# Linear attention and routed experts: the first LayerNorm's statistics move from VectorE to ScalarE

## The chip, the cores and the metric

The kernel runs on one core of a Trainium2 chip (trn2). The metric is device time in microseconds (us); the time before is the median of three runs. PE is TensorE, DVE is VectorE, ACT is ScalarE, POOL is GpSimd and SP is SyncE, whose queue issues most transfers.

## What is computed

The input x has 8 sequences of 512 tokens and 256 features. In short:

```
def _layernorm(x, axis=-1, eps=1e-05):
    m = jnp.mean(x, axis=axis, keepdims=True)
    v = jnp.var(x, axis=axis, keepdims=True)
    return (x - m) / jnp.sqrt(v + eps)
...
    x = L0_attn_x
    x = x + _L0_attn_ref(_layernorm(x, axis=-1), ...)
    x = x + _L0_ffn_ref(_layernorm(x, axis=-1), ...)
    return x
```

The attention is a causal linear one: q, k and v are projected, phi(z) = elu(z) + 1 is taken of q and k, running sums of k*v and of k decay with a constant for each head, and q times the first is divided by the sum over the head of q times the second; then comes the output projection. The second part routes each token to 4 of 32 small gated experts and adds one shared expert. The change concerns the LayerNorm ahead of the attention only.

## The kernel before

The kernel has two phases. The first is a software pipeline of nine steps, b = 0 to 8, written out by hand (`steps(step)` on each engine). In step b the engines do, for one sequence each: the attention of sequence b (`st.now`), the output projection, second LayerNorm and router of sequence b-1 (`st.before`), the placing of the rows of sequence b-2 in lists for the experts (`st.past`), and the first LayerNorm of sequence b+1 (`st.after`, steps 0 to 6). Before step 0 the first LayerNorm of sequence 0 is done alone. Beside it three experts' weights are turned in each step: PE transposes them into three PSUM banks in turn, ACT copies the high half out, DVE the low half (`prep_in`, `prep_out`; L720 and L875). The second phase runs tiles of 128 rows through the experts (32 of the shared expert and 159 of routed ones), and a last part adds three partial sums and stores the output. The change touches nothing behind the first phase.

Every engine works through its own list in order; semaphores tie the lists together. A sequence is held as 128 partitions x 4 tiles (TS = 4) x 256 features.

The first LayerNorm of sequence b+1 before the change: at the top of its step DVE runs `bn_stats` on four tiles (L798) and `bn_aggr` four times (L801), with two small writes between that carry waits (L315), and writes the variance plus epsilon (`vare`, L805) and minus the mean (`less`, L807). POOL raises the variance to the power -0.5 (L573) and multiplies by `less` (`shift`, L577); that is `root(0, b+1)`. ACT then writes the normalised rows `xn` in four instructions (L706, `norm_in`), PE transposes them (L1129, `xn_in`) and ACT copies the result out as `xnT` (L711, `xn_out`). The next step's projections (L1261) start from it.

What stands around it in the order of the lists, for a step b with all parts:

- ACT: exp and relu of k, feature half 0 (L726, L727); the spread of the inverted denominators (L743); the same two of q (L733, L734); `share_out` (L698); `norm_in(b+1)` (L706); the issue of the load of x for sequence b+2 (L756); k and q, half 1, and the copies of the turned weights.
- DVE: statistics of b+1; `choose` (L965, L967); the attention output (L890); `count_rows` (L973 to L979); phi of half 0 (L851, L853), the scan (L859) and k*v (L865); the residual sum (L903, once for each half of the rows); the second LayerNorm's statistics (L798 again); `rank_picks` (L989 on), weights (L875), the second LayerNorm itself (L823), the split of its rows (L845), and the second half of the attention with its scans (L870) and the inversion (L835, L837); router selection (L947, L950).
- PE: denominators (L1361), q projection, transposes of the spread denominators (L1285), v projection, output projection (L1296, 16 matmuls, which wait for L890), then K, Q and V of half 1 with weight transposes between (L1139 to L1144), `xn_in`, more weights, the next K, and the router's transposes and matmuls (L1330, L1348).
- POOL: in steps 3 to 8 it issues the indirect transfers that put rows in the experts' lists (L586), in fixed numbers between its other work: 3, then `root(0, b+1)`, 3, then q*ksum (L562), 2, then `root(1, b-1)` for the second LayerNorm (L573 again), and more around the two products q*kvsum (L566).
- SP: the store of the residual rows, which the second LayerNorm waits for, and the loads of the next experts' weights (L366 to L370), for which the first weight transpose of a step waits.

Of the kernel before, what the change touches and what calls it, by code (L numbers as in the profile page):

```python
# [5 lines left out]
def moe_block(nc, x, w_qkv, w_out, decay_param, router_w, router_b, gate_w, up_w, down_w,  # L6
              shared_gate_w, shared_up_w, shared_down_w, w_late, out):
    f32, f16, i32, u32 = mybir.dt.float32, mybir.dt.float16, mybir.dt.int32, mybir.dt.uint32
    ALU = mybir.AluOpType
# [3 lines left out]
    P = 128  # L13
# [3 lines left out]
    TS = S // P  # L17
# [31 lines left out]
    with ctx:  # L49
        def sb(name, shape, dt):  # L50
            return ctx.enter_context(nc.sbuf_tensor(name, shape, dt))
# [4 lines left out]
        def sem(name):  # L56
            return ctx.enter_context(nc.semaphore(name))
# [98 lines left out]
        idx8 = sb("idx8", [P, TS, 8], u32)  # L156
        carrier = sb("carrier", [P, 1], f32)
        iota_i = top8[:, :, :].rearrange("p j k -> p (j k)").bitcast(i32)
        iota_e = sb("iota_e", [P, E], f32)
# [21 lines left out]
        row_experts = payload[:, :, EXP_AT // 2 - H:EXP_AT // 2 - H + K]  # L181
        share_sum = sb("share_sum", [P, TS], f32)
        mhalf = sb("mhalf", [P, TS], f32)
        stats = [sb(f"stats{n}", [P, TS, 6], f32) for n in range(2)]
        mv = [sb(f"mv{n}", [P, TS, 2], f32) for n in range(2)]
        vare = [sb(f"vare{n}", [P, TS], f32) for n in range(2)]
# [32 lines left out]
        setup_dve = sem("setup_dve")  # L219
        ln_stats = [sem(f"ln_stats{n}") for n in range(2)]  # L220
        ln_aggr = [sem(f"ln_aggr{n}") for n in range(2)]
        ln_vare = [sem(f"ln_vare{n}") for n in range(2)]
# [89 lines left out]
        def wait_apart(eng, semaphore, value):  # L312

            eng.wait_ge(semaphore, value)
            nc.vector.memset(carrier[:, :], 0.0)  # L315
# [329 lines left out]
        def _(act):  # L645
# [49 lines left out]
            def share_out(b):  # L695

                act.wait_ge(share_shifted, b + 1)
                nc.scalar.activation(shares, shares, ACT.Exp).then_inc(share_exp, 1)  # L698

            def norm_in(b):  # L700

                act.wait_ge(ln_shift, b + 1)
                if b >= 1:
                    act.wait_ge(xn_transposed, HC * b)
                for j in range(TS):
                    nc.scalar.activation(xn[:, j], x_sb[b % 2][:, j], ACT.Identity, bias=shift[:, j:j + 1], scale=rstd[0][:, j:j + 1]).then_inc(xn_ready, 1)  # L706
# [29 lines left out]
            def step(st):  # L736
                b = st.b
                if st.now:
                    k_parts(b, 0)
                if st.before:  # L740

                    act.wait_ge(den_inverted, b)
                    nc.scalar.activation(attn_words.rearrange("p (n d) -> p n d", d=D), rden[:, :].unsqueeze(2).to_broadcast([P, TS * HEADS, D]), ACT.Copy).then_inc(rden_spread, 1)  # L743
                if st.now:
                    q_parts(b, 0)
                if st.past:
                    share_out(b - 2)
# [35 lines left out]
                if st.now:  # L783
                    for n in range(6, 9):
                        prep_out(b, n)

            norm_in(0)
            xn_out(0)
# [6 lines left out]
        def _(dve):  # L795
            def norm_stats(n, src, b):
                for j in range(TS):
                    nc.vector.bn_stats(stats[n][:, j], src[:, j]).then_inc(ln_stats[n], 1)  # L798
                wait_apart(dve, ln_stats[n], TS * b + TS)
                for j in range(TS):  # L800
                    nc.vector.bn_aggr(mv[n][:, j], stats[n][:, j]).then_inc(ln_aggr[n], 1)  # L801
                if n == 0 and b >= 1:
                    dve.wait_ge(ln_shift, b)
                wait_apart(dve, ln_aggr[n], TS * b + TS)
                nc.vector.tensor_scalar(vare[n][:, :], mv[n][:, :, 1], LN_EPS, None, ALU.add).then_inc(ln_vare[n], 1)  # L805
                if n == 0:
                    nc.vector.tensor_scalar(less, mv[0][:, :, 0], -1.0, None, ALU.mult).then_inc(ln_less, 1)  # L807

            dve.wait_ge(x_loaded[0], 16)
            norm_stats(0, x_sb[0], 0)  # L810
            dve.wait_ge(setup_act, 4)
# [7 lines left out]

            def norm(n, dst, src, b, done):  # L820
                dve.wait_ge(ln_rstd[n], b + 1)
                for j in range(TS):
                    nc.vector.tensor_scalar(dst[:, j], src[:, j], mv[n][:, j, 0:1], rstd[n][:, j:j + 1],  # L823
                                            ALU.subtract, ALU.mult).then_inc(done, 1)
# [52 lines left out]
            def step(st):  # L877
                b = st.b
                if st.after:
                    dve.wait_ge(x_loaded[(b + 1) % 2], 16 * ((b + 1) // 2 + 1))  # L880
                    norm_stats(0, x_sb[(b + 1) % 2], b + 1)
                if st.past:
# [8 lines left out]
                if st.past:  # L891
                    count_rows(b - 2)
                if st.now:
                    phi(b, 0)
                    k_sum(b, 0)
                    k_times_v(b, 0)
                if st.before:
# [7 lines left out]
                    dve.wait_ge(x1_done, 2 * b)  # L905
                    norm_stats(1, x1_sb, b - 1)
                if st.past:
# [8 lines left out]
                if st.before:  # L916
                    dve.wait_ge(x1_stored, 16 * b)
                    norm(1, xn2, x1_sb, b - 1, xn2_ready)
                if st.now:
# [489 lines left out]
```

## Time and profile before

| | |
|---|---|
| median of 3 runs | 755.38 us (753.37 to 756.12) |
| span of the profiled execution, first to last instruction | 707.9 us |
| what the median has around that span | 47.5 us |
| PE busy | 603.2 us (85%) |
| DVE busy | 512.6 us (72%) |
| ACT busy | 434.9 us (61%) |
| POOL busy | 440.3 us (62%) |

The spans come from one execution that the hardware profiler recorded; no separate device time of that execution is given, so its span stands beside the median. Busy shares are averages over both phases. In the first phase, up to about 280 us, the engines take turns in waiting for each other, and what one of them saves counts only where the chain of waits goes through it.

### The profile page before, as it was taken

The numbers are of one execution on the slowest core, as the hardware profiler recorded it, in microseconds if no ns is written. First come the engines' busy times: TensorE is split into PE (matmuls) and PEld (weight loads), VectorE is DVE, ScalarE is ACT, GpSimd is POOL, SyncE is SP. The second block draws the span as 40 slices with busy tenths as digits, with TensorE's granted clock in tenths as the row PEclk, the third lists the DMA queues.
The fourth block names the chain that finished last, engine by engine and source line by source line (L and its number), as shares of the span: only waits on it lengthen the run. The fifth ranks groups of instructions, "written<-read, shape, count | busy, mean of one in ns | idle before, by whom it ended". The sixth has DMA issues, their size and how long they took to land.

```text
span 707.9 us, 15496 instructions
## 1 busy us (share of the span) xinstructions
PE 603.2 (85%) x4725; PEld 417.4 (59%) x4725; DVE 512.6 (72%) x1966; ACT 434.9 (61%) x1045; POOL 440.3 (62%) x367
## 2 busy tenths in 40 slices
PE   3898877897888899899999999999999999999000
PEld 2565544565555565677777777776777777776000
DVE  2588898989889968877766666666666666666164
ACT  2646445463636433688878878787788878788000
POOL 3031148658585776777078778887888888888300
PEclk9989999899999969999999999999999999999555
DMA  9664585959667676999589889888988888886799
GB/s 275 265 182 120 160 240 176 301 194 271 197 203 226 202 229 205 302 335 336 164 148 144 139 140 143 140 141 140 143 140 149 140 140 142 141 145 91 189 412 385
DMA packets 121460, 140.41 MB, mean 198 GB/s; under 512 B 22626, under 2 KB 110210, under 8 KB 120834
## 3 DMA queue, kind: packets, MB, share of 16 engines
q1 hardware_dynamic: 88816, 97.29, 44.4%
q0 software_dynamic: 29040, 38.68, 33.1%
q10 hardware_dynamic: 3522, 3.44, 1.5%
q8 instruction: 40, 0.66, 0.4%
q14 instruction: 42, 0.34, 0.2%
HBM read 79.19 MB, written 64.89 MB: 204 GB/s over the span
## 4 chain that ended last, share of the span: by engine, by line
PE 60%; DVE 19%; issue 6%; DMA 6%; POOL 4%; SPq 3%; ACT 2%; POOLq 0%; ACTq 0%; DVEq 0%
PE psD L1245 13%; PE psQ L1212 11%; PE psK L1212 11%; PE psT L1183 6%; PE psD L1296 4%; DMA acc_scratch<-arena 3%; DVE W L875 2%; DVE W L870 2%; SPq L514 2%; PE psK L1261 2%; PE psQ L1261 2%; DMA W<-acc_scratch 2%; PE psT L1232 2%; PE psV L1261 2%; PE psV L1232 2%
## 5 line engine op out<-in xcount | busy, mean ns | idle before, releaser
L640 POOL DMA_INDIRECT acc_scratch<-arena x159 | 251.3, 1581 | 73.2 <-issue 34.7
L586 POOL DMA_INDIRECT xlist_scratch<-list_row,dest x128 | 133.7, 1045 | 35.6 <-issue 34.1
L1245 PE MATMUL psD<-W,arena 128*128 (+1 forms) x955 | 135.5, 273 | 1.0 <-DVE arena L1044 0.9
L1048 DVE COPY arena<-psT 128x512 f16<-128x512 f16 x191 | 81.0, 424 | 69.2 <-PE psT L1183 68.6
L1212 PE MATMUL psK<-W,arena 128*128 (+1 forms) x576 | 109.3, 326 | 0.5 <-DVE arena L1048 0.5
L1212 PE MATMUL psQ<-W,arena 128*128 (+1 forms) x570 | 108.2, 326 | 0.1
L1245 PEld LDWEIGHTS psD<-W,arena 128*128 128x128 f16 x955 | 85.2, 98 | 8.0 <-DVE arena L1044 1.1
L671 ACT ACTIVATE arena<-arena 128x192 f16<-128x192 f32 x191 | 69.2, 362 | 13.9 <-DVE arena L1072 2.2
L680 ACT ACTIVATE arena<-psD,arena 128x256 f32<-128x256 f32 x159 | 72.8, 458 | 3.4 <-DMA acc_scratch<-arena 3.1
L1183 PE MATMUL psT<-ident,arena 128*128 128x128 f16 x764 | 74.0, 220 | 0.4 <-issue 0.4
L1183 PEld LDWEIGHTS psT<-ident,arena 128*128 128x128 f16 x764 | 57.0, 98 | 29.3 <-issue 7.2
L1091 DVE TENSOR_TENSOR arena<-arena 128x64 f16<-128x64 f32 x191 | 43.0, 225 | 40.4 <-ACT arena L671 40.4
L1212 PEld LDWEIGHTS psK<-W,arena 128*128 128x128 f16 x576 | 50.6, 97 | 33.7 <-DVE arena L1048 1.1
L1212 PEld LDWEIGHTS psQ<-W,arena 128*128 128x128 f16 x570 | 50.1, 97 | 32.4 <-DVE arena L1048 0.2
L566 POOL TENSOR_TENSOR W<-W 128x512 f32<-128x512 f32 x16 | 20.3, 1270 | 71.4 <-DVE W L870 71.3
L1092 DVE TENSOR_TENSOR arena<-arena 128x128 f16<-128x128 f32 x191 | 54.4, 285 | 0.0
L668 ACT ACTIVATE arena<-psT 128x384 f16<-128x384 f16 x95 | 46.6, 490 | 10.0 <-PE psT L1232 5.6
L668 ACT ACTIVATE arena<-psV 128x384 f16<-128x384 f16 x96 | 47.0, 490 | 7.4 <-PE psV L1232 2.1
L875 DVE SCALAR_TENSOR_TENSOR W<-psT,W 128x384 f16<-128x384 f32 (+1 forms) x72 | 40.0, 588 | 13.6 <-ACT W L720 13.6
L1296 PE MATMUL psD<-W 128*128 128x256 f32 x128 | 36.3, 447 | 11.6 <-DVE W L890 11.5
L720 ACT ACTIVATE W<-psT 128x384 f16<-128x384 f32 (+1 forms) x72 | 35.6, 528 | 16.5 <-PE psT L1139 8.5
L664 ACT ACTIVATE arena<-psK 128x192 f32<-128x192 f32 x96 | 31.7, 330 | 20.4 <-PE psK L1212 20.0
(164 smaller groups left out, 1084.8 us busy)
## 6 DMA issues: line engine op xcount, KB each, us to landing
arena<-xlist_scratch SPq DMA_DIRECT2D x159, 136.0 KB
W<-acc_scratch SPq DMA_DIRECT2D x24, 512.0 KB, 12.7
acc_scratch<-arena SPq DMA_DIRECT2D x16, 512.0 KB, 5.9
arena<-in_L_attn_x_dram SPq DMA_DIRECT2D x10, 512.0 KB, 5.1
arena<-in_L_ffn_down_w_dram SPq DMA_DIRECT2D x23, 192.0 KB, 4.9
xlist_scratch<-pad_scratch SPq DMA_DIRECT2D x32, 136.0 KB, 3.6
list_row<-xrow_scratch SPq DMA_DIRECT2D x32, 136.0 KB
acc_scratch<-arena SPq DMA_DIRECT2D x33, 128.0 KB, 12.4
```

Source lines behind the costliest of these rows:

```text
L586: nc.gpsimd.indirect_dma_start(xlist[:, :], bass.IndirectOffsetOnAxis(ap=dest[:, n:n + 1], axis=0), list_row[j % LISTS][:, :], None).then_ ...
L640: nc.gpsimd.indirect_dma_start(acc[t % ACCS][:, :], bass.IndirectOffsetOnAxis(ap=token[:, (t - NT) % DEEP:(t - NT) % DEEP + 1], axis=0), y ...
L668: nc.scalar.activation(aT[u].rearrange("p n t -> p (n t)"), psA[u], ACT.Copy).then_inc(aT_done, 1)
L671: nc.scalar.activation(halves[t % 2][:, 0:I], act32[t % 2], ACT.Copy).then_inc(a_hi_done, 1)
L680: nc.scalar.activation(y_sb[(t - 2) % ROUND], psY[t % 2], ACT.Copy, scale=share[:, (t - 2 - NT) % DEEP:(t - 2 - NT) % DEEP + 1]).then_inc( ...
L875: nc.vector.scalar_tensor_tensor(dst, bank_of("prep", n)[:, 0:width], WS, hi, ALU.mult, ALU.subtract).then_inc(prep_lo, 1)
L1048: nc.vector.tensor_copy(xT[t % 2].rearrange("p s c t -> p (s c t)"), psX[t % 2]).then_inc(xT_done, 1)
L1092: nc.vector.tensor_tensor(both[:, 2 * P:3 * P], act32[t % 2][:, 0:P], both[:, 0:P], ALU.subtract).then_inc(a_split, 1)
L1183: last = nc.tensor.transpose(psX[t % 2][:, n * P:(n + 1) * P], xg[t % XG][:, n * P:(n + 1) * P], ident16[:, :])
L1212: last = nc.tensor.matmul(psG[t % 2][:, 0:GU], xT[t % 2][:, sx, h], weights(t, (2 * h + sw) * GU, GU), start=(n == 0), stop=(n == 3 * HC - 1))
L1245: last = nc.tensor.matmul(psY[u], aT[u][0:height, part], weights(t - 2, GUW + q * H, H, height), start=(n == 0), stop=(n == len(parts) - 1))
L1296: last = nc.tensor.matmul(psD[:, j // 2, (j % 2) * H:(j % 2 + 1) * H], attnT[:, c, j * P:(j + 1) * P], wout_sb[:, c, :], start=(c == 0), s ...
```

## The change

ACT now makes the statistics of the first LayerNorm. `sum_in` copies each tile of x into `xn`, used as scratch, and lets ACT's accumulator add it up (four instructions); DVE turns the sums into minus the mean (`mean_in`, one operation on 128 x 4). `square_in` squares x minus the mean with the accumulator on (four instructions); DVE turns these into variance plus epsilon (`variance_in`, one operation). POOL's two operations and ACT's `norm_in` stay. The second LayerNorm keeps `bn_stats` on DVE.

In the lists, ACT gets `sum_in(b+1)` between L727 and L743 and `square_in(b+1)` between L734 and L698; DVE has `mean_in(b+1)` at the top of the step, where the statistics stood, and `variance_in(b+1)` behind `count_rows`, ahead of phi. For sequence 0 all four parts stand in front of everything else of the pipeline, on ACT behind the four set-up operations L652 to L655.

```
+            def sum_in(b):
+                act.wait_ge(x_loaded[b % 2], 16 * (b // 2 + 1))
+                if b >= 1:
+                    act.wait_ge(xn_transposed, HC * b)
+                    act.wait_ge(ln_less, b)
+                for j in range(TS):
+                    nc.scalar.activation(xn[:, j], x_sb[b % 2][:, j], ACT.Copy, accum_out=x_sum[:, j:j + 1]).then_inc(x_summed, 1)
+
+            def square_in(b):
+                act.wait_ge(ln_less, b + 1)
+                if b >= 1:
+                    act.wait_ge(ln_vare[0], b)
+                for j in range(TS):
+                    nc.scalar.activation(xn[:, j], x_sb[b % 2][:, j], ACT.Square, bias=less[:, j:j + 1],
+                                         accum_out=x_square[:, j:j + 1]).then_inc(x_squared, 1)
...
                 if st.now:
                     k_parts(b, 0)
+                if st.after:
+                    sum_in(b + 1)
                 if st.before:
...
                 if st.now:
                     q_parts(b, 0)
+                if st.after:
+                    square_in(b + 1)
...
+            sum_in(0)
+            square_in(0)
             norm_in(0)
...
+            def mean_in(b):
+                if b >= 1:
+                    dve.wait_ge(ln_shift, b)
+                    dve.wait_ge(xn_ready, TS * b)
+                dve.wait_ge(x_summed, TS * b + TS)
+                nc.vector.tensor_scalar(less, x_sum, -1.0 / H, None, ALU.mult).then_inc(ln_less, 1)
+
+            def variance_in(b):
+                dve.wait_ge(x_squared, TS * b + TS)
+                if b >= 1:
+                    dve.wait_ge(ln_rstd[0], b)
+                nc.vector.tensor_scalar(vare[0][:, :], x_square, 1.0 / H, LN_EPS, ALU.mult, ALU.add).then_inc(ln_vare[0], 1)
...
-            dve.wait_ge(x_loaded[0], 16)
-            norm_stats(0, x_sb[0], 0)
+            mean_in(0)
+            variance_in(0)
...
                 if st.after:
-                    dve.wait_ge(x_loaded[(b + 1) % 2], 16 * ((b + 1) // 2 + 1))
-                    norm_stats(0, x_sb[(b + 1) % 2], b + 1)
+                    mean_in(b + 1)
...
                 if st.past:
                     count_rows(b - 2)
+                if st.after:
+                    variance_in(b + 1)
                 if st.now:
                     phi(b, 0)
```

## Rows read from the trace of the kernel before

**Rows 1.** The chain that ended last, step 4: start, us, what.

```profile
134.38 1.30 DVE stats L798 x4
136.64 1.20 DVE W L890 x2
151.24 0.79 DVE arena L823 x3
```

**Rows 2.** PE's timeline, steps 2, 3, 4: start, us, engine, line, shape, [idle before <-releaser].

```profile
73.96 5.34 PE L1296 MATMUL psD<-W 128*128 128x256 f32 x16 [2.19 <-DVE W L890]
81.28 0.49 PE L1139 MATMUL psT<-ident,arena 128*128 128x128 f32 x3
...
105.03 3.72 PE L1296 MATMUL psD<-W 128*128 128x256 f32 x16 [2.20 <-DVE W L890]
...
133.81 1.88 PE L1261 MATMUL psV<-W 128*128 128x512 f32 x4
137.88 5.41 PE L1296 MATMUL psD<-W 128*128 128x256 f32 x16 [2.19 <-DVE W L890]
```

**Rows 3.** Stretches: us, PE, PEld, DVE, ACT, POOL busy, PEclk, DMA share, GB/s.

```profile
140.00:141.00 1.00, 1.00 (x4) 0.81 (x3) 1.00 (x2) 1.00 (x3) 0.78 (x1) 0.50 0.68 252
252.00:256.00 4.00, 4.00 (x17) 3.19 (x16) 0.62 (x1) 0.00 (x0) 3.79 (x4) 0.50 0.12 37
```

**Rows 4.** ACT's timeline, steps 2 and 4.

```profile
67.84 1.06 ACT L743 ACTIVATE W<-W 128x1024 f32<-128x1024 f32 x1 [1.99 <-DVE W L837]
...
131.76 1.06 ACT L743 ACTIVATE W<-W 128x1024 f32<-128x1024 f32 x1 [1.53 <-DVE W L837]
139.98 0.60 ACT L706 ACTIVATE W<-arena,W,rstd 128x256 f32<-128x256 f32 x1 [3.17 <-POOL W L577]
```

**Rows 5.** POOL's timeline, step 4, and DVE's in step 3.

```profile
138.22 1.12 POOL L573 TENSOR_TENSOR rstd<-vare,mhalf 128x4 f32<-128x4 f32 x1
147.69 1.04 POOL L573 TENSOR_TENSOR rstd<-vare,mhalf 128x4 f32<-128x4 f32 x1
...
119.93 1.54 DVE L823 TENSOR_SCALAR arena<-arena,mv,rstd 128x256 f32<-128x256 f32 x4 [2.04 <-POOL rstd L573]
```

**Rows 6.** Groups by line and shape: x count, busy us, mean ns, idle before.

```profile
L680 ACT ACTIVATE arena<-psD,arena 128x256 f32<-128x256 f32 x159 | 72.8, 458 | 3.4 <-DMA acc_scratch<-arena 3.1
L706 ACT ACTIVATE W<-arena,W,rstd 128x256 f32<-128x256 f32 x32 | 16.6, 592 | 19.2 <-POOL W L577 19.2
L1057 DVE DVE_READ_ACCUMULATOR arena<-arena 128x1 f32 x159 | 13.2, 83 | 0.0
L682 ACT ACTIVATE arena<-psD 128x256 f32<-128x256 f32 x32 | 11.8, 369 | 2.3 <-DMA acc_scratch<-arena 2.3
L698 ACT ACTIVATE payload<-payload 128x16 f32<-128x16 f32 x8 | 1.7, 216 | 18.4 <-DVE payload L965 18.4
```

**Rows 7.** Timeline of the start, before step 0.

```profile
6.89 0.17 DVE L805 TENSOR_SCALAR vare<-mv 128x4 f32<-128x4 f32 x1
8.33 0.20 POOL L577 TENSOR_TENSOR W<-W,rstd 128x4 f32<-128x4 f32 x1
9.96 0.24 ACT L655 ACTIVATE rwT<-psD 128x64 f16<-128x64 f32 x1
10.07 2.08 ACT L706 ACTIVATE W<-arena,W,rstd 128x256 f32<-128x256 f32 x4
```

**Rows 8.** Timeline of step 0.

```profile
19.23 0.59 ACT L727 ACTIVATE W<-psK 128x512 f32<-128x512 f32 x1
21.76 2.06 ACT L706 ACTIVATE W<-arena,W,rstd 128x256 f32<-128x256 f32 x4
```

**Rows 9.** DVE's timeline in step 1.

```profile
43.52 1.29 DVE L890 TENSOR_TENSOR W<-W,psD 128x512 f32<-128x512 f32 x2 [0.24 <-PE psD L1285]
```

**Rows 10.** SP's queue in step 2, and transfers of 62 to 82 us.

```profile
73.41 0.47 SPq L370 DMA_DIRECT2D arena<-in_L_ffn_down_w_dram  x1
...
arena<-in_L_ffn_down_w_dram SPq DMA_DIRECT2D x3, 64.0 KB, 4.7
```

More of the change, by code:

```diff
@@ L157, in moe_block @@
         carrier = sb("carrier", [P, 1], f32)
+        stats_words = sb("stats_words", [P, 2 * TS], f32)
         iota_i = top8[:, :, :].rearrange("p j k -> p (j k)").bitcast(i32)
@@ L182, in moe_block @@
         share_sum = sb("share_sum", [P, TS], f32)
+        x_sum, x_square = stats_words[:, 0:TS], stats_words[:, TS:2 * TS]
         mhalf = sb("mhalf", [P, TS], f32)
-        stats = [sb(f"stats{n}", [P, TS, 6], f32) for n in range(2)]
-        mv = [sb(f"mv{n}", [P, TS, 2], f32) for n in range(2)]
+        stats = sb("stats", [P, TS, 6], f32)
+        mv = sb("mv", [P, TS, 2], f32)
         vare = [sb(f"vare{n}", [P, TS], f32) for n in range(2)]
@@ L219, in moe_block @@
         setup_dve = sem("setup_dve")
-        ln_stats = [sem(f"ln_stats{n}") for n in range(2)]
-        ln_aggr = [sem(f"ln_aggr{n}") for n in range(2)]
+        ln_stats, ln_aggr = sem("ln_stats"), sem("ln_aggr")
+        x_summed, x_squared = sem("x_summed"), sem("x_squared")
         ln_vare = [sem(f"ln_vare{n}") for n in range(2)]
@@ L795, in _, with norm_stats @@
         def _(dve):
-            def norm_stats(n, src, b):
+            def mean_in(b):
[9 more added lines that the diff above has]
+                nc.vector.tensor_scalar(vare[0][:, :], x_square, 1.0 / H, LN_EPS, ALU.mult, ALU.add).then_inc(ln_vare[0], 1)
+            def norm_stats(src, b):
                 for j in range(TS):
-                    nc.vector.bn_stats(stats[n][:, j], src[:, j]).then_inc(ln_stats[n], 1)
-                wait_apart(dve, ln_stats[n], TS * b + TS)
+                    nc.vector.bn_stats(stats[:, j], src[:, j]).then_inc(ln_stats, 1)
+                wait_apart(dve, ln_stats, TS * b + TS)
                 for j in range(TS):
[L801 to L807, printed above, removed]
-            dve.wait_ge(x_loaded[0], 16)
-            norm_stats(0, x_sb[0], 0)
+                    nc.vector.bn_aggr(mv[:, j], stats[:, j]).then_inc(ln_aggr, 1)
+                wait_apart(dve, ln_aggr, TS * b + TS)
+                nc.vector.tensor_scalar(vare[1][:, :], mv[:, :, 1], LN_EPS, None, ALU.add).then_inc(ln_vare[1], 1)
+            mean_in(0)
+            variance_in(0)
             dve.wait_ge(setup_act, 4)
@@ L818, in _, with norm @@
             dve.wait_ge(setup_dve, 3)
-            def norm(n, dst, src, b, done):
-                dve.wait_ge(ln_rstd[n], b + 1)
+            def norm(dst, src, b, done):
+                dve.wait_ge(ln_rstd[1], b + 1)
                 for j in range(TS):
-                    nc.vector.tensor_scalar(dst[:, j], src[:, j], mv[n][:, j, 0:1], rstd[n][:, j:j + 1],
+                    nc.vector.tensor_scalar(dst[:, j], src[:, j], mv[:, j, 0:1], rstd[1][:, j:j + 1],
                                             ALU.subtract, ALU.mult).then_inc(done, 1)
@@ L905, in step @@
                     dve.wait_ge(x1_done, 2 * b)
-                    norm_stats(1, x1_sb, b - 1)
+                    norm_stats(x1_sb, b - 1)
                 if st.past:
@@ L917, in step @@
                     dve.wait_ge(x1_stored, 16 * b)
-                    norm(1, xn2, x1_sb, b - 1, xn2_ready)
+                    norm(xn2, x1_sb, b - 1, xn2_ready)
                 if st.now:
```

## The prediction

> **What bounds the kernel now.** I read the page first: PE is busy most and DVE next, but both are averages over two phases, and the change lies in the first. So I followed the chain of waits through that phase, then laid the timelines of PE, ACT, DVE and POOL of one step beside each other, and last asked for short stretches to see PE's granted clock.
>
> In step 4 the chain goes through the four `bn_stats` at the top of DVE's step, from 134.38, and reaches the attention output L890 at 136.64 [rows 1]. PE waits 2.19 us for it in front of the output projection, though its v projection (four matmuls of 0.43, so 1.72 of path) had begun at 133.81 and is over near 135.6 [rows 2]. From L1296 on PE is busy without a gap until the weights' transposes, and then the chain is DVE's again from the second LayerNorm L823 at 151.24 [rows 1] to the next step's statistics. So the statistics lie on the path, at 134.38 to 136.4. Steps 2, 5 and 6 read the same. Three steps differ. In step 1 DVE waits for PE before L890 [rows 9], so the statistics before it cost nothing. In step 3 POOL is last: L823 waits 2.04 us for POOL's root [rows 5]. Steps 7 and 8 have no first LayerNorm.
>
> A second effect lies on the same place. L1296 takes 5.34 and 5.41 us in steps 2 and 4 but 3.72 in step 3 [rows 2], and the clock granted at 140 to 141 is 0.50 [rows 3]: the 1.2 GHz level, granted for 3.4 us after PE had stood idle. The wait for DVE thus costs about 1.8 us more in steps 2, 4, 5 and 6.
>
> **The price of the new ACT operations.** No ACT instruction of the trace uses the accumulator. A tile of 128x256 costs 369 ns without a pointer operand, 458 with one (its scale), 592 with two [rows 6]. Four L706 in a row take 2.08 us [rows 7], or 0.50 each, so neighbours overlap by 0.1. A copy is then 0.28 and a square with its bias pointer 0.36, if reading the accumulator is hidden: the lower ends. If the read is an instruction of its own, the nearest rows are DVE's read, 83 ns, and a tiny ACT operation, 216 ns [rows 6]; with 216 and no overlap the copy is 0.59 and the square 0.67: the upper ends. I take a little above the middle, 0.45 and 0.54: a read without much to do, partly overlapped. Four and four make 1.8 and 2.2 us (1.1 to 2.4, and 1.4 to 2.7).
>
> The Trainium skill, ScalarE: Activation LUTs, section What ACT_TABLE_LOAD costs, gives 186 ns plus 0.833 per element, 93 more for a pointer operand, and an overlap of 93. By it a copy is 0.31 and a square 0.40, an estimate without the accumulator's read; the eight would be 2.8 us instead of my 4.0. The rows at 369 and 458 are near it (399 and 493), and it has no price for the read.
>
> **The start: +6.0 us.** Now DVE and POOL finish the statistics of sequence 0 at 8.53 under ACT's idle wait, and ACT goes from its set-up operation at 9.96 straight to L706 at 10.07 [rows 7]. With the change ACT can begin to sum only at 10.07, as its queue is in order. Then come 1.8 for the sums, 0.3 for `mean_in` with the hand-over both ways (an operation on 128x4 is 0.17), 2.2 for the squares, 0.25 for `variance_in`, and POOL's pair, 1.47 from L805's end to L577's end [rows 7]: 6.0 us until L706 can start. The cover that hid this work is gone, and PE has nothing else to do. Ends: 4.5 and 7.1.
>
> **Step 0: +2.5 us.** In it ACT goes from L727 at 19.23 over q to L706 at 21.76, without a wait for POOL [rows 8]. Now the sums run from 19.7 to 21.5, q to 22.5, squares to 24.7, DVE's variance to 25.0, POOL to 26.5, and `norm_in` starts 4.7 late. Queued behind it on ACT are k and q of half 1 and the weights' copies; queued behind `variance_in` on DVE is phi of half 0, so V of half 1 on PE waits too. PE's transposes of xn come about 1.9 late, ACT's copies of them and the next K 2.5 late; idle time of PE absorbs the rest. Ends: 1.1 and 3.6, as the eight prices change.
>
> **Step 1: 0.** It is PE-bound [rows 9]. The sums fit between L727 and L743, as PE and DVE are slower here. The squares end about 0.8 behind L890 and hold phi back by that; DVE waits for PE in L903 anyway.
>
> **Step 2: -2.8 us.** DVE loses 1.97 of statistics and gets `mean_in` for 0.1. PE's end is limited by the spread L743: ACT idles 1.99 in front of it, where step 4 has 1.53 [rows 4], and with the overlap of 0.1 the 1.8 of sums fit in. L1296 starts 1.9 earlier, with 0.3 of idle time before it. Then the 1.2 GHz stretch should not come, which gives 1.8 more. But then a transfer is in the way: the last weights are issued at 73.41 plus 0.47 and take 4.7 to land [rows 10], so 78.6, while the first weight transpose, L1139 at 81.28 now [rows 2], would come 3.7 earlier, at 77.6. It waits 1.0. So 1.9 + 1.8 - 1.0, near 2.8. Without the clock it is 1.9.
>
> **Step 3: 0.** POOL is last, and its list of work is the same; `variance_in` at about 104.5 is there before POOL asks for it.
>
> **Steps 4, 5, 6: -2.4 us each.** The sums push L743 back by 1.8 - 1.63 = 0.2 in step 4; PE still starts L1296 about 1.9 earlier. With the clock 3.7 would be free, but POOL is next: its second L573 ends at 147.69 + 1.04 = 148.73 [rows 5], and its chain of work up to there has no gap since DVE's scan at the end of the step before. L823 can go from 151.24 [rows 1] to 148.83, which is 2.4. Without the clock 1.9 counts in full. The squares run 134.6 to 136.8, DVE asks for them at 137.3, POOL for the variance at 138.22 [rows 5], and L706 stays near 139.98 [rows 4], ahead of the k it stands before. Ends of the price: at 0.67 a square the last is there at 137.3, still in time; at 0.59 a sum L743 is 0.7 late, and L1296 gains 1.5 before the clock.
>
> **Sum.** 6.0 + 2.5 - 2.8 - 7.2 = -1.5 us against the profiled span of 707.9, so 706.4. The median of the runs, 755.38, has 47.5 around that span, which the change doesn't touch: 753.9 us. With the low prices it is -1.5 - 1.5 - 1.4 = -4.4 (751.0), with the high ones -1.5 + 1.1 + 1.1 + 1.2 = +1.9 (757.3).
>
> **Rivals.**
> - *The clock stays low in the steps.* 6.0 + 2.5 - 4 x 1.9 = +0.9: 756.3. For it: the idle wait for L743 stays. Against: the low stretch came right behind the 2.19 of idle time, and that is what goes.
> - *The clock at the phase's end.* At 252 to 256 the granted clock is 0.50 while PE is wholly busy [rows 3]. PE fills and computes the last denominators there on the path, some 13 us of such work before the last residual sum; I estimate 5 of them to be the clock's, as L1296 loses 1.7 of 5.4 to it [rows 2] and this stretch is three times as long. Whether a drop falls there seems to hang on where the timeline lies. Shifted, it may not come: 753.9 - 5 = 749.
> - *The accumulator is dear (the other side).* If every accumulated instruction drains ACT, at 0.8 for a sum and 0.9 for a square, the start is 3.2 + 3.6 + 2.1 = 8.9, step 0 is 2.5 + 2.8 = 5.3, and L743 is pushed 1.1 late in steps 2, 5 and 6 and 1.6 in step 4, so that L1296 gains 1.1, 1.1, 1.1 and 0.6. Sum +10.3: 765.7. It turns the sign from a mean price of 0.59 on and shows as slower by over 0.5% from about 0.70. Against it: a tiny ACT operation is only 216 ns.
> - *The accumulator is free:* 751.0, above.
> - *Tables.* Square could need another activation table than Exp. The trace has one load of 1.3 us at the start and one in the second phase, so exp, relu and copies share one now. Two loads of 1.3 in each of eight LayerNorms, half of them hidden, would be +10: 764. The Trainium skill, ScalarE: Activation LUTs, section Table sets: the hidden batching unit, says that cheap functions are in every set and that a switch is about 2.7 us; by it sixteen switches would be 43 us of ACT, an estimate, if Square were no such function. No row here has a Square.
>
> **How the numbers follow.** Forecast 0.50; clock stays low in the steps 0.10; clock at the end comes back 0.15; accumulator free 0.10; accumulator dear 0.12; tables 0.03. A change within 0.5%, or 3.8 us, is about what a measurement here can't tell from none: 751.6 to 759.2. Faster: 0.15, and 0.06 of the free accumulator, and 0.04 of the forecast, make 0.25. Slower: 0.12 + 0.03 + 0.02 = 0.17. The rest, 0.58, is no change. The range runs from 747, below the end-clock case, to 760, above the high prices with the low clock; it leaves out the dear accumulator and the tables, 0.15.
>
> **What would show it.** Right: `norm_in(0)` starting at 16 instead of 10.07; step 0 some 2.5 longer; PE idle before L1296 near 0.3 in steps 2, 4, 5, 6 and its 16 matmuls near 3.6; L823 of steps 4 to 6 waiting for POOL's L573; four sums in 1.8 and four squares in 2.2. Wrong: L1285 waiting longer for L743 than its 0.75 to 1.5 of now; DVE waiting at `variance_in` in steps 2 to 6; table loads between the steps; another clock pattern in step 1 or 8, which alone can move the time by 3 to 5 us.

## The result, and the profile after

The changed kernel takes 757.39 us (20 runs, 751.26 to 761.04), the kernel before 750.38 (20 runs beside them, 744.66 to 756.12): a ratio of 1.0087, 95% interval 1.0061 to 1.0113, so it is slower by 6.5 us. The forecast was 753.9 and most likely no change; the range of 747 to 760 holds the time, the sign does not fit. That the range holds it is luck: the forecast started from 755.38, the median of three runs, where 20 runs give 750.38, and put the change at -1.5, where it is +6.5. Two errors of 5 and 8 us went against each other.

Two things about the comparison first. The profiled execution of after spans 759.2 us and its own time was 761.04, so only 1.8 us lie around a span (1.7 to 1.9 in every later run). The 707.9 of before was thus an execution near 710, and the 47.5 us that the forecast added were no constant. Chips differ: on some the kernel before takes 703 to 706 us, on others 750 to 752, nearly all of it in the first tiles of the second phase (last section). Ratios below are always against the kernel before on the same chip, and steps are compared in the first phase only, where the profiles of both kinds of chip show the same step lengths.

Each step is timed at the start of the second LayerNorm's normalisation (L823 before, L860 after), which stands in the last part of a step. The table has these starts in us, from the timelines of two executions of each kernel; the rows "later than before" are what the change had cost up to there:

```
step                     1       2       3       4       5       6       7       8
before, first         56.18   87.25  119.93  151.24  182.39  213.51  241.53  272.64
after, first          63.00   91.83  124.07  155.43  186.14  216.86  246.85  277.21
later than before      6.8     4.6     4.1     4.2     3.8     3.4     5.3     4.6
before, second        56.59   87.73  120.40  150.74  180.31  211.55  239.55  267.50
after, second         63.15   90.89  123.09  153.42  183.29  213.98  243.97  272.05
later than before      6.6     3.2     2.7     2.7     3.0     2.4     4.4     4.6
```

Both pairs tell one story: 6.7 lost until step 1, 2.2 and 3.4 won back in step 2, 1.2 and 0.7 in all of steps 3 to 6, and 2 lost again in step 7. The forecast ran +8.5 up to step 1, then -2.8, 0, three times -2.4, 0.

The start, after (timeline; the rows that answer to [rows 7] and [rows 8]):

```profile
9.92 0.44 ACT L709 ACTIVATE W<-arena 128x256 f32<-128x256 f32 x1
...
11.87 0.51 ACT L717 ACTIVATE W<-arena,W 128x256 f32<-128x256 f32 x1 [0.24 <-DVE W L828]
...
14.23 1.04 POOL L575 TENSOR_TENSOR rstd<-vare,mhalf 128x4 f32<-128x4 f32 x1 [9.10 <-DVE vare L835]
...
15.66 2.07 ACT L726 ACTIVATE W<-arena,W,rstd 128x256 f32<-128x256 f32 x4 [1.72 <-POOL W L579]
...
32.48 0.60 ACT L726 ACTIVATE W<-arena,W,rstd 128x256 f32<-128x256 f32 x1 [2.56 <-POOL W L579]
```

ACT starts to sum when it started to normalise before, and normalises 5.6 later, at 15.66. In step 0 the second row of L726 stands at 32.48; it was 21.76, so 10.7 later, 5.1 of it new.

The new operations, after: ACT's timeline at the start of step 5, and the groups (line, shape, count, busy, mean ns):

```profile
165.31 0.43 ACT L709 ACTIVATE W<-arena 128x256 f32<-128x256 f32 x1
165.62 0.21 ACT L709 ACTIVATION_READ_ACCUMULATOR W<-arena 128x1 f32 x1
165.71 0.42 ACT L709 ACTIVATE W<-arena 128x256 f32<-128x256 f32 x1
...
167.92 1.06 ACT L765 ACTIVATE W<-W 128x1024 f32<-128x1024 f32 x1 [0.91 <-DVE W L874]
```
```profile
L717 ACT ACTIVATE W<-arena,W 128x256 f32<-128x256 f32 x32 | 15.9, 503 | 1.6 <-DVE W L828 0.9 <-issue 0.7
L709 ACT ACTIVATE W<-arena 128x256 f32<-128x256 f32 x32 | 12.9, 419 | 0.0
L709 ACT ACTIVATION_READ_ACCUMULATOR W<-arena 128x1 f32 x32 | 6.6, 205 | 0.0
L717 ACT ACTIVATION_READ_ACCUMULATOR W<-arena,W 128x1 f32 x32 | 6.2, 195 | 0.0
```

The read is an instruction of 0.2 us, but the next one starts 0.09 behind it: a sum costs 0.40 from start to start (165.31 to 165.71), a square 0.49. The Trainium skill (ScalarE: Activation LUTs, What ACT_TABLE_LOAD costs) gives the figures from which the prediction worked out 0.31 and 0.40, an estimate without the read. The trace agrees: from the start of a copy to that of its read it is 0.31, and the 0.09 comes on top. No table load was added: both traces have two, one at 2.75 and one in the second phase.

PE after, steps 2 and 5 (answers to [rows 2]), and the granted clock (answers to [rows 3]):

```profile
78.75 3.72 PE L1334 MATMUL psD<-W 128*128 128x256 f32 x16 [0.17 <-DVE W L926]
...
85.81 0.55 PE L1177 MATMUL psT<-ident,arena 128*128 128x128 f32 x3 [1.19 <-DMA arena<-in_L_ffn_down_w_dram]
...
163.62 3.42 PE L1399 MATMUL psD<-W 128*128 128x8 f32 x16
166.89 3.76 PE L1299 MATMUL psQ<-W 128*128 128x512 f32 x4
170.44 1.86 PE L1323 MATMUL psD<-ident,W 128*128 128x128 f32 x8
```
```profile
160.00:164.00 4.00, 3.61 (x39) 3.17 (x36) 3.97 (x6) 2.47 (x6) 0.00 (x0) 0.73 1.06 312
164.00:168.00 4.00, 4.00 (x17) 3.48 (x17) 3.38 (x6) 3.09 (x12) 3.63 (x3) 0.50 0.85 248
168.00:172.00 4.00, 4.00 (x12) 2.34 (x11) 2.72 (x20) 2.29 (x4) 3.33 (x5) 0.50 1.10 284
```

Step 2 has the mechanism of the forecast: the output projection comes after 0.17 of idle time (0.3 forecast) and at 2.4 GHz, and the weights' transpose waits 1.2 for its transfer (1.0 forecast). In step 5 the clock is low in another place, from 162 to 172: the denominators take 3.42 instead of 1.92, q 3.76 instead of 1.96. The chain that ended last has moved there:

```profile
163.82 3.21 PE psD L1399 x16
167.04 3.61 PE psQ L1299 x4
170.65 1.67 PE psD L1323 x8
172.34 1.29 DVE W L926 x2
```

DVE had waited 0.55 for the denominators (L872) and waits 1.6 more for PE at the attention output (now L926), together more than the 1.9 that it saved. Denominators of 3.42 stand in steps 4, 5, 6 and 7 of this execution and in 4, 6 and 7 of the second, where L926 waited 0.56, 1.22 and 1.21. The kernel before had such slow denominators in one step of each of its two executions.

PE is not the only wait in these steps. The rest of step 4, on DVE and POOL:

```profile
144.27 0.16 DVE L835 TENSOR_SCALAR vare<-stats_words 128x4 f32<-128x4 f32 x1
144.52 1.41 POOL L575 TENSOR_TENSOR rstd<-vare,mhalf 128x4 f32<-128x4 f32 x1 [2.19 <-DVE vare L835]
150.44 1.40 DVE L844 TENSOR_SCALAR vare<-mv 128x4 f32<-128x4 f32 x1
150.52 1.28 POOL L564 TENSOR_TENSOR W<-W 128x512 f32<-128x512 f32 x1
154.28 1.04 POOL L575 TENSOR_TENSOR rstd<-vare,mhalf 128x4 f32<-128x4 f32 x1
155.43 1.54 DVE L860 TENSOR_SCALAR arena<-arena,mv,rstd 128x256 f32<-128x256 f32 x4
```

The change put `variance_in` (L835) behind L926 and `count_rows`. So when PE holds L926 back, POOL's first root waits too, 2.19 here and 1.2 to 1.6 in the other slow steps, and its whole list moves with it: the second root ends at 155.32, and L860 starts at 155.43. Before the change the statistics stood ahead of L890, and in steps 3 to 6 POOL waited for no variance. Beside this DVE loses 1.2: a 128x4 operation that takes 0.17 elsewhere takes 1.40 and ends 0.03 behind POOL's q*ksum product; the chain that ended last runs through it. Each of steps 4 to 6 has one such operation with the change and none before it (there they stand in steps 3 and 7). DVE and POOL come out within 0.1 of each other, so neither alone is what L860 waits for. No run moved `variance_in`.

The second execution has one step among 4 to 7, step 5, with fast denominators, and shows what is next. POOL and DVE in it (answers to [rows 5]):

```profile
162.17 1.27 POOL L568 TENSOR_TENSOR W<-W 128x512 f32<-128x512 f32 x1 [4.71 <-DVE W L907]
...
169.46 1.26 POOL L588 DMA_INDIRECT xlist_scratch<-list_row,dest  x1 [0.31 <-issue]
...
172.25 1.73 POOL L575 TENSOR_TENSOR rstd<-vare,mhalf 128x4 f32<-128x4 f32 x1
...
182.14 1.04 POOL L575 TENSOR_TENSOR rstd<-vare,mhalf 128x4 f32<-128x4 f32 x1
```
```profile
183.29 1.22 DVE L860 TENSOR_SCALAR arena<-arena,mv,rstd 128x256 f32<-128x256 f32 x3 [1.54 <-POOL rstd L575]
```

POOL works from 162.17 to 183.18, 21.0 us, where the kernel before took 20.05 for the same list. The root took 1.73 instead of 1.12 and two list transfers 0.3 more. All 17 profiles give the root's price by its neighbour: 1.71 to 1.73 where DVE's scan (L896 in the changed kernel) runs as it starts (24 times), 1.37 to 1.41 beside phi (L888, L890; 43 times), 1.01 to 1.14 in all other places (194 times). With the statistics gone DVE is earlier in its list, so POOL's root meets the scan. So the step lasts 29.87, not the 28.7 to 28.9 that the forecast's -2.4 leaves, which was POOL's bound; and the kernel before, when no low stretch hit it, made step 5 in 29.57.

### The profile page after: what moved, and what is told of

Its sections match the earlier page's. It is cut to its first block, busy times and chain, and to the rows that moved or that the text cites. A ratio compares the mean times of both kernels' runs of the same rounds, so it can differ in the third digit from the quotient of the medians.

```text
span 759.2 us, 15565 instructions
## 1 busy us (share of the span) xinstructions
PE 620.5 (82%) x4725; PEld 427.4 (56%) x4725; DVE 500.2 (66%) x1886; ACT 465.1 (61%) x1173; POOL 441.3 (58%) x367
## 4 chain that ended last, share of the span: by engine, by line
PE 58%; DVE 16%; another core or an unknown queue 5%; issue 5%; DMA 5%; ACT 3%; SPq 3%; POOL 3%; ACTq 0%; POOLq 0%; DVEq 0%
PE psD L1283 13%; PE psK L1250 12%; PE psQ L1250 12%; PE psT L1221 6%; PE psT L1270 2%; SPq L516 2%; DVE W L912 2%; PE psV L1270 2%; DMA W<-acc_scratch 2%; PE psQ L1299 2%; PE psD L1399 2%; POOL xlist_scratch L588 2%; DVE arena L882 1%; DVE arena L860 1%
## 5 line engine op out<-in xcount | busy, mean ns | idle before, releaser
L1283 PE MATMUL psD<-W,arena 128*128 (+1 forms) x955 | 137.6, 276 | 6.6 <-DVE arena L1082 6.6
L1250 PE MATMUL psK<-W,arena 128*128 (+1 forms) x576 | 111.4, 330 | 14.4 <-DVE arena L1086 14.4
L1250 PE MATMUL psQ<-W,arena 128*128 (+1 forms) x570 | 111.4, 333 | 9.3 <-issue 9.3
L1221 PEld LDWEIGHTS psT<-ident,arena 128*128 128x128 f16 x764 | 58.0, 99 | 32.3 <-issue 10.9
L666 ACT ACTIVATE arena<-psQ 128x192 f32<-128x192 f32 x95 | 31.4, 331 | 40.6 <-remote 19.2
```

What stands on the lines that cost most here:

```text
L666: nc.scalar.activation(gate, psG[t % 2][:, 0:I], ACT.Silu, scale=1 / WS).then_inc(silu_done, 1)
L1221: last = nc.tensor.transpose(psX[t % 2][:, n * P:(n + 1) * P], xg[t % XG][:, n * P:(n + 1) * P], ident16[:, :])
L1250: last = nc.tensor.matmul(psG[t % 2][:, 0:GU], xT[t % 2][:, sx, h], weights(t, (2 * h + sw) * GU, GU), start=(n == 0), stop=(n == 3 * HC - 1))
L1283: last = nc.tensor.matmul(psY[u], aT[u][0:height, part], weights(t - 2, GUW + q * H, H, height), start=(n == 0), stop=(n == len(parts) - 1))
```

## Experiments

Theory A: the start and step 0 cost what they should, some 8 us, and the gain of steps 4 to 6 went to two things, a low clock on the denominators and, behind it, POOL. Rivals stand in the expectations. The runs were made on four chips, at most four kernels beside the kernel before on each. Where two ratios are compared, the +- is worked out from their two 95% intervals, and the two can come from different chips.

**The two kernels again, for second profiles.**

> The kernel before, unchanged, for a second profile and for the scatter. Theory A (the start and step 0 of the change cost 5.6 and 2.8 us, and of the gains of steps 2 to 6 the clock takes most back): the time is that of the kernel before, ratio 1.000 within 0.004; the profile shows the output projection of steps 2, 4, 5, 6 behind some 2.2 us of idle time, part of them at 1.2 GHz, and the denominators and q projection of most steps at 2.4 GHz. It also shows whether the span of 707.9 us, 43 below the median time, was a usual one: if PE stands still for tens of us in the first tiles of the second phase, it was not. Rival B (the change is slower only by its start): the same.

Ratio 0.9987 (0.9955 to 1.0019) against itself, 703.99 us, and the profile spans 702.8: no standstill in the second phase on this chip. Denominators were slow in one step (4), the output projection in three (2, 3 and 6).

> The changed kernel again, beside the others on this chip. Both theories: 1.009 of the kernel before (1.006 to 1.012), 6 to 8 us. Theory A: the denominators and the q projection again at 1.2 GHz in steps 4, 5 and 6, so that a step lasts about 30.7 us instead of the 28.7 that it would take at 2.4 GHz. Rival B: the low stretches fall elsewhere in this execution, and the steps come out shorter.

1.0105 (1.0070 to 1.0140). Steps 4 and 6 as expected at 30.3 and 30.7; step 5 fast and 29.87, above the 28.7 expected: that is where POOL showed.

**Undoing the start, then step 0.** Statistics of sequence 0, then of 0 and 1, back on DVE:

```
-            sum_in(0)
-            square_in(0)
...
-            mean_in(0)
-            variance_in(0)
+            early_in(0)          # the old bn_stats, bn_aggr, vare and less
```

> The change with sequence 0 alone left on VectorE, as before: the work in front of step 0 is undone, steps 0 to 6 stay changed. Theory A: 5.6 us less than the changed kernel, so about +1.5 us against the kernel before, ratio 1.002; first transposes of xn back at 12 us. Rival B (the loss is in the steps, since the clock is slow there, and the start is made up by something behind it): the ratio stays above 1.006.

1.0014 (0.9982 to 1.0047), 0.0091 +- 0.0048 below the unaltered change. ACT's first normalisation is back:

```profile
9.90 2.08 ACT L728 ACTIVATE W<-arena,W,rstd 128x256 f32<-128x256 f32 x4
```

> Sequences 0 and 1 left on VectorE, so that the start and step 0 are those of the kernel before and only steps 1 to 6 have the new order. Theory A: 2.5 us less again: ratio 0.998 to 0.999, which is the net gain of the steps alone, about -1 us, where DVE's saved 1.9 us in each of steps 2, 4, 5, 6 would make -7.6. Rival B: 1.004 or more. Rival C (the clock's loss in the steps comes from the later start, by where the timeline lies): the steps get their 1.9 us each, ratio 0.990.

0.9976 (0.9947 to 1.0005). By the ratios the start is worth 6.4 us and step 0 2.7, near theory A's 5.6 and 2.8; the second alone is not clear of noise (0.0038 +- 0.0044), the two together, 9.1 us, are. The steps alone are thus worth -1.7 us (-3.7 to +0.4), not the -10 that the forecast had for them. Rival C falls: with the start of the kernel before, the denominators were slow in steps 5, 6 and 7 again.

**A fill that keeps PE busy.** Dummy matmuls whose result nobody reads:

```
+                elif st.before:
+                    pe.wait_ge(kv_done, HC * b)
+                    hold_clock(5)                    # ahead of the spread denominators' transposes
...
+                    if st.before:
+                        pe.wait_ge(x1_done, 2 * b)
+                        hold_clock(2, psD[:, 1, :])  # ahead of the router's transposes
...
+                        if j == 2 and st.after:
+                            hold_clock(3, psD[:, 1, :])
```

> The changed kernel with dummy matmuls where PE stands idle in steps 1 to 7: five of 512 columns behind the q projection (while it waits for the spread denominators), and two and three in the router's stage. Nothing else waits for them. Theory A (low clock on denominators and q projection takes the steps' gain): the denominators' 16 matmuls take 1.9 us instead of 3.4 in all steps, steps 4 to 6 last as long as POOL lets them, 29.9 us instead of 30.7, and step 7 is 2 us shorter: 1.004 of the kernel before against 1.010 without the fill. Rival B (PE is not what a step waits for, the low clock there is hidden): the clock changes, the time doesn't, 1.010. Rival C (the fill delays the router and the output projection): over 1.012.

1.0102 (1.0048 to 1.0156), where 1.004 was expected: a miss, the time did not move. Steps 4 to 6 did as expected, 30.3, 30.1 and 29.9 us with fast denominators:

```profile
165.56 1.85 PE L1407 MATMUL psD<-W 128*128 128x8 f32 x16
167.26 1.96 PE L1299 MATMUL psQ<-W 128*128 128x512 f32 x4
169.06 1.24 PE L1292 MATMUL psV<-W,ident 128*128 128x512 f16 x5
```

But in step 1 the fill stood at 1.2 GHz, 2.34 us long, in front of work that waited, and its step 1 ended 2.5 later than that of the change's second execution, step 2 another 1.0. By step 7 the fast steps had made up all but 0.75 of this; then step 8, with a low stretch of 3.4 us, took 31.9, where the change had 30.4 and 28.1. And POOL was in the way of more: L860 waited 1.55 for the root in each of steps 4 to 6.

> The same fill with sequences 0 and 1 on VectorE. Theory A: the start's 8 us less: 0.991 to 0.993. Rival B: 0.998.

0.9942 (0.9896 to 0.9989), 0.1 to 0.3% behind the expectation, and not clear of the 0.9976 without the fill (0.0034 +- 0.0055).

> The kernel before with eight dummy matmuls in steps 2 to 7 where PE waits 2.2 us for the attention output, into a PSUM bank that is free then. Tells what the low clock cost the kernel before. Theory A: the output projection takes 3.7 us in all steps instead of 5.4 in three or four of them: 3 to 6 us less, ratio 0.992 to 0.996. If the ratio is 1.000, the clock's loss was hidden before, and the change gave up nothing there.

```
+                elif st.past:
+                    pe.wait_ge(k_acted, HC * b + 1)
+                    hold_clock(8, psK[:, :])         # while the attention output is awaited
```

1.0056 (1.0007 to 1.0106): a miss. The output projection ran at 2.4 GHz in every step from 2 on, and the denominators were slow in two steps, 4 and 6, where the kernel before has one in each of its profiles:

```profile
187.78 3.42 PE L1364 MATMUL psD<-W 128*128 128x8 f32 x16
191.06 3.76 PE L1261 MATMUL psQ<-W 128*128 128x512 f32 x4
```

This looks like the change's own effect, made without the change: PE's idle time ahead of the output projection is gone, and two long low stretches (13.7 and 10.2 us) begin in the router's stage or right behind it and cover the denominators, for which DVE waits 1.2 and 0.7 at L835. One profile, with two such steps against one, suggests this and does not prove it.

**POOL's list.** Two list transfers go behind the second LayerNorm's root:

```
-                    list_some(3, 6)
+                    list_some(3, 5)
...
-                    list_some(6, 8)
+                    list_some(5, 6)
...
-                    list_some(8, 11)
+                    list_some(6, 11)
```

> As the run with sequences 0 and 1 on VectorE and the fill, and POOL issues two of its list transfers behind the second LayerNorm's root instead of ahead of it (five instead of eight stand between the two roots' places... three stand ahead of q*ksum and the root where five stood). Theory A: POOL is the next bound of steps 4 to 6 at 29.9 us; its root comes 2.5 us earlier and the steps fall to 28.2 to 28.5: 4 us less than without it, ratio 0.986. Rival B (another wait stands right behind POOL's, such as DVE's own work): no more than 1 us less.

0.9860 (0.9814 to 0.9905), 0.0082 +- 0.0065 below the run without POOL's edit. Steps 4 to 6 take 28.9, 28.3 and 28.3 us, and no low stretch lies between 43 and 261.

```profile
152.88 1.85 PE L1422 MATMUL psD<-W 128*128 128x8 f32 x16
...
160.80 3.72 PE L1352 MATMUL psD<-W 128*128 128x256 f32 x16 [0.16 <-issue]
```

> The kernel before with POOL's list transfers moved as in the last run (two of them behind the second LayerNorm's root) and nothing else. POOL was last in step 3 only. Theory A: step 3's wait of 2.0 us for the root goes, the steps 4 to 6 stay at 29.6 to 31.2 as DVE's: 0.997. Rival (the order of POOL alone made the gain of the last run): 0.99 or less.

0.9995 (0.9955 to 1.0035). Step 3's wait fell from 2.04 to 0.28, and step 4, with slow denominators, took 32.0 instead of 31.3 and 30.3. The rival, 0.99 or less, falls.

> Sequences 0 and 1 on VectorE, POOL's transfers moved, no fill. Theory A: the low clock on denominators and q projection is what the steps wait for, so POOL's relief helps in step 3 (2.5 us) and not in those steps that lie at 1.2 GHz: 0.993 to 0.995, against 0.986 with the fill. Rival (POOL was what mattered): 0.988.

0.9924 (0.9897 to 0.9951), at the better end of the 0.993 to 0.995 expected: three steps still had slow denominators (4, 6 and 7), at 30.0 to 31.3 us, and step 5 without them took 28.5 from one L860 to the next. POOL's edit alone is thus worth 0.0052 +- 0.0040 of the time, some 2.5 us of it in step 3, and the fill on top of it 0.0064 +- 0.0052.

> The kernel before with POOL's transfers moved and the fill of the router and of the wait for the spread denominators in steps 3 to 7. It tells whether ScalarE's statistics have any part in the gain of the best version. Theory A: DVE is last at 29.6 us a step, less the low stretches: 0.993. If it comes out at 0.986 the statistics might as well have stayed.

1.0056 (1.0024 to 1.0087), where 0.993 was expected: a miss. With the statistics on DVE POOL's order and this fill together give nothing: PE waits its 2.19 ahead of the output projection, and low stretches stand there in steps 3, 5 and 6. Against the next run, which differs in the statistics alone, that is 0.0145 +- 0.0045, so in this company the change is worth 10.9 us. What was not run is the kernel before with POOL's order and a fill in all three places, ahead of the output projection too.

> Sequences 0 and 1 on VectorE, POOL's transfers moved, fill in steps 3 to 7 only. The fill cost steps 1 and 2 some 3 us in the runs before, as it stood in front of work that PE could have done. Theory A: 0.982 to 0.985 of the kernel before, steps 4 to 6 at 28.3 us, step 2 back at 27.5. Rival (the fill of step 2 kept a low stretch away from step 3): no better than 0.986.

0.9911 (0.9879 to 0.9943), a miss against 0.982 to 0.985. Steps 5 to 7 ran at 28.3, 28.3 and 27.4, but some 3 us behind the first fill of a router's stage, which is step 3's, came a low stretch of 10 us over step 4's denominators. That fits the rival, that the fill of the steps before was worth its cost, but the time does not settle it: 0.9911 is not clear of the 0.9860 with the early fill nor of the 0.9924 with none.

**The fill and POOL on the unaltered change.**

> The changed kernel as it is, and the fill in steps 3 to 7 only, so that steps 1 and 2 are free of its cost. Theory A (the low clock on the denominators and the q projection, and behind it POOL, took the gain of steps 4 to 6): steps 4 to 6 at 29.9 us, no denominators at 3.4 us in them, step 7 at 28; about 3 to 4 us under the changed kernel, 1.004 to 1.006. Rival D (the position of the timeline alone decides, fill or not): one or two of steps 4 to 6 at 30.7 with low denominators.

1.0089 (1.0045 to 1.0133), above the expectation of 1.004 to 1.006, which its interval still holds. Steps 4 to 6 at 30.6, 29.9 and 29.9 with fast denominators and L860 waiting 1.5 for POOL in each, so rival D falls; a low stretch of 14 us came in step 8, as in the first execution of before; step 8 took 31.1, where the change had 30.4 and 28.1.

> The same with POOL's two transfers moved. Theory A: steps 4 to 6 at 28.3 us, step 3 2.5 us shorter, 7 to 8 us less than the run before this one: 0.993 to 0.996. That is the whole gain that was forecast for the steps, and more, on the kernel with its late start. Rival D: 1.000 or more.

0.9999 (0.9964 to 1.0034), by the ratios 0.9% or 6.3 us below the run above (0.0090 +- 0.0056). Steps 4 to 6 took 28.6, 28.3 and 28.4:

```profile
159.70 1.91 PE L1407 MATMUL psD<-W 128*128 128x8 f32 x16
...
167.93 3.72 PE L1337 MATMUL psD<-W 128*128 128x256 f32 x16 [0.16 <-DVE W L926]
```

The total was 0.4 to 0.7% above the expectation, so in time a miss, on the edge of rival D's 1.000; by its steps, all fast, rival D falls. This profile shows two low stretches of 6.8 us in steps 1 and 2, which may be the difference.

> The changed kernel with the fill of the router's stage alone (two and three matmuls in steps 3 to 7), none in the wait for the spread denominators. Theory A: it is the router's stage, with its small transposes and waits, behind which the clock falls, so that these five suffice: denominators at 1.9 us in steps 4 to 7. Rival E (it is the 0.9 to 1.5 us of waiting for the spread denominators): the low stretches stay.

716.08 us in a single run, which says nothing within 1%. In its profile, with the fill in the router's stage alone, the denominators of steps 4 to 7 took 1.85 to 1.92 us, and rival E falls as far as one execution goes. Three low stretches of 3.4 us still came between 190 and 225.

## Why the prediction was wrong

- **Prices of the ACT operations.** Forecast 0.45 and 0.54, measured 0.40 and 0.49. Right, within the bounds.
- **The start, +6.0.** 5.6 in the profile, 6.4 when undone. Right, in mechanism too.
- **Step 0, +2.5.** Denominators start at 43.91 instead of 35.52, which is 8.4, less 5.6: 2.8 (1.9 in the second pair); undone, 2.7. Right.
- **Step 1, 0.** It gained 1.6 and 1.0. In the first pair the low stretch there lasts 3.4 us instead of 6.8. In the second pair both have 3.4; there PE had waited 0.87 for DVE's L890 in the kernel before, so the step was not PE-bound as [rows 9] made it seem.
- **Step 2, -2.8.** -2.2 and -3.4. Right, with the clock's part and the transfer's.
- **Step 3, 0.** -0.4 and -0.5. Right.
- **Steps 4, 5, 6, -2.4 each.** This is the step that failed. Measured 0, -0.4, -0.4 and 0, +0.3, -0.6. The forecast had these steps fall from 31.1 to 31.3 us to 28.7 to 28.9; they took 30.7 to 31.4 and 29.9 to 30.7. Two of its terms were wrong, and they cover each other.
  - *The clock.* "The 1.2 GHz stretch should not come" was half a truth: it left the output projection and came to the denominators. I had seen that the low clock follows PE's idle time, and had taken it that less idle time means less of it. The runs showed a second place, the router's stage with its short transposes and waits; when the clock falls there, low stretches of 10 us or more cover the denominators, q and the spread's transposes. DVE waits for the first (0.5 to 1.2) and again, now 1.9 us earlier, for the last (0.6 to 1.6). With the statistics on DVE the second wait is covered, the first is not: the slow steps of the kernel before and of its two variants with POOL's edit or the fill (five in steps 4 to 6) took 30.3 to 32.0, never with a wait of the attention output for PE, against 29.6 where neither place was slow. So the fall is dear in either kernel; what the change did is to have it in two or three of these steps instead of in one or none.
  - *POOL's bound*, 28.7 to 28.9, was too low: with fast denominators the step takes 29.9, as POOL's list took 1.0 longer. The forecast took its prices over as they were, but in the fast steps its root now runs beside DVE's scan and costs 1.7 instead of 1.1. In steps with slow denominators the list is held back by `variance_in` as well, a wait that the forecast took to be nothing.
  - *Which counts for how much.* The fill alone brings the three steps from 92.8 and 90.9 us to 90.3. POOL's edit on top brings them to 85.2; the forecast had 86.4. So with the clock high POOL's 4 us remain, and with POOL's edit but no fill (90.1, on the version with an early start) the clock's remain. Putting right only one of the two terms would still have left the forecast wrong.
  - *The base.* All three steps of the profile that the forecast started from had a low stretch on the output projection (31.1 to 31.3). Where there was none, in step 5 of the second execution, the kernel before took 29.6, less than the change's 29.9. So part of the 2.4 was there to be won only in some executions.
- **Step 7, no change.** +2.0 in both pairs: it has no first LayerNorm, but slow denominators reach it all the same. With fast ones it took 27.9 and 28.5 (the two fills on the change), as before.
- **The rival "clock stays low in the steps"** named the right engine, but its price was +0.9 over the time before, by gains of 1.9 in four steps, three of which did not have them; its 756.3 lies near the measured 757.39 only by the base that was 5 too high. Its chance, 0.10, was too small for what the clock did.

With steps 4 to 7 put in as measured (-0.5 and +2.0, means of the two pairs), the forecast's own sum is 6.0 + 2.5 - 2.8 - 0.5 + 2.0 = 7.2, where the ratios say 6.5 and 7.4. That it agrees is in part luck, as the gains of steps 1 and 3, 1.3 and 0.5, are left out; with them it is 5.4. The table above ends 4.6 later in both pairs, and the spans of the second pair differ by 5.0; a single execution of each is not the median, and what makes up the other 2 is open.

What stays open: why the fall lands on the router's stage in some steps and on the output projection in others. Filling one place only left it in the other; the position in time seems to play a part, as two executions of one kernel differ in it. Open too is what `variance_in` ahead of L926 would give in the slow steps.

**The better version.** Statistics of sequences 0 and 1 on DVE, the rest on ACT, POOL's two transfers moved and the fill in steps 1 to 7: 0.9860, so 10.5 us less than the kernel before and, by the ratios, 17 less than the change as made.

## What to carry over

An engine that works ahead of a pipeline's first step pays for the whole of a moved piece of work once, uncovered; leave the first rounds as they were. Before counting what a freed engine gains in a steady step, price the other engines' path at the low clock of TensorE too, above all where TensorE does many short things between waits, and price the second bound in its new company: POOL's root cost 1.0 to 1.7 us by what VectorE did beside it. And look at what now stands behind what: a small operation put behind a long wait passes the wait on. A gain of 2 us in each step was there, but needed two further edits: a fill to hold the clock, which by itself gave nothing clear of noise, and a few of POOL's transfers behind what the others wait for, which by itself gave 0.5%.

## What the runs showed of the hardware

ScalarE's accumulator read is an instruction of its own: 205 ns busy, 90 ns of path.

VectorE and GpSimd slow each other on small operations. GpSimd's 128x4 power costs 1.0 to 1.1 us, 1.4 beside VectorE's phi and 1.7 beside its scan. A VectorE operation on 128x4 or 128x16, 0.17 otherwise, takes up to 1.9 us when a 128x512 product of GpSimd runs, and then ends 0.03 to 0.04 behind it. Both are read from the timelines; no run was made for them.

The 45 us between chips lie near the start of the second phase. PE's busy time there, in two executions of the changed kernel, the first on a chip of the slower kind (stretch, PE, PEld, DVE, ACT, POOL busy, clock, DMA share, GB/s):

```profile
285.00:300.00 15.00, 7.24 (x39) 3.38 (x37) 4.07 (x24) 2.19 (x4) 11.55 (x13) 0.73 0.74 234
300.00:315.00 15.00, 1.04 (x7) 0.50 (x6) 2.58 (x9) 0.90 (x3) 8.41 (x9) 0.50 0.25 93
```
```profile
281.00:296.00 15.00, 13.31 (x122) 9.22 (x119) 13.54 (x57) 9.88 (x29) 11.76 (x13) 1.00 0.87 289
296.00:311.00 15.00, 13.99 (x132) 10.34 (x131) 10.94 (x36) 12.11 (x34) 11.35 (x13) 1.00 1.00 320
```

In the first, PE is busy for 8.3 of 30 us, and the chain of waits puts 39.9 us between 250 and 400 down to "another core or an unknown queue", mostly waits of 5 to 8 us. All nine profiles on slower chips have 30 to 45 us of it, the eight on faster ones none. What is waited for there no row says.
